# Band masks of a local attention brought to PSUM by 64x64 tiles of the array instead of full 128x128 matmuls

## The reference

```python
def local_attention(q, k, v):
    ...
    sim = jnp.einsum('bhwid,bhwjd->bhwij', bq, bk)
    mask = (i < j) | (i > j + WINDOW) | (j == -1)
    sim = jnp.where(mask, -jnp.finfo(sim.dtype).max, sim)
    attn = jax.nn.softmax(sim, axis=-1)
    out = jnp.einsum('bhwij,bhwjd->bhwid', attn, bv)

def _layer(x, wqkv, qs, ksc, wo, lg, lb, w1, b1, w2, b2):
    q, k, v = jnp.split(shift_token(x) @ wqkv, 3, axis=-1)
    q, k = rotary_xpos(l2norm(q) * qs, l2norm(k) * ksc)
    x = x + local_attention(q, k, v) @ wo
    a, g = jnp.split(layernorm(shift_token(x)) @ w1 + b1, 2, axis=-1)
    return x + (a * gelu(g)) @ w2 + b2

x = x + 0.5 * _L0_ffn_ref(_layernorm(x), ...)
x = x + _L0_attn_ref(_layernorm(x), ...)
x = x + 0.5 * _L0_ffn_ref(_layernorm(x), ...)
```

## Time and profile before

| | |
|---|---|
| median of three runs | 2494.72 us (2492.01 to 2496.49) |
| the profiled execution | 2494.18 us |
| its span in the trace | 2492.4 us |
| mean granted clock of TensorE | 0.952 |
| busy: PE, PE weight loads, DVE, ACT, POOL | 2238.0, 1670.2, 1709.9, 1465.2, 1095.6 us |
| first matmul of q and k in the two calls of the feed-forward stage | 67.63 and 1287.17 us |

### The profile page before, as it was taken

The page is one execution under the profiler, slowest core; times in us unless marked ns, Lnnn a source line. Parts: engine busy times, 40 slices in busy tenths (PEclk is TensorE's granted clock), DMA queues, the critical chain, the costliest instruction groups (busy, mean ns, idle before and its releaser), DMA issues. The chain is left out here.

```text
span 2492.4 us, 52712 instructions
## 1 busy us (share of the span) xinstructions
PE 2238.0 (90%) x21606; PEld 1670.2 (67%) x21606; DVE 1709.9 (69%) x2815; ACT 1465.2 (59%) x2389; POOL 1095.6 (44%) x800
## 2 busy tenths in 40 slices
PE   1799999999999969999969999999999997597968
PEld 1577777777777646666646777777777775495758
DVE  3677777778888636777737777777788784563556
ACT  0476767666676515555546677766676664363635
POOL 4655555656555210000025565656555560550245
PEclk8799999999999969999989999999999998698979
DMA  7000000069999970000000000000000002221022
GB/s 152 1 1 1 2 1 1 1 76 119 131 147 147 147 85 1 2 2 2 2 1 1 2 1 1 1 2 2 1 2 1 1 1 68 55 70 38 33 74 81
DMA packets 211362, 90.88 MB, mean 36 GB/s; under 512 B 79700, under 2 KB 206721, under 8 KB 210996
## 3 DMA queue, kind: packets, MB, share of 16 engines
q1 hardware_dynamic: 202596, 72.27, 21.8%
q0 software_dynamic: 6080, 11.76, 1.5%
q10 hardware_dynamic: 2448, 3.48, 0.7%
HBM read 24.51 MB, written 63.41 MB: 35 GB/s over the span
## 5 line engine op out<-in xcount | busy, mean ns | idle before, releaser
L477 POOL TENSOR_TENSOR work<-work,rot_tables 128x512 f32<-128x512 f32 x256 | 446.5, 1764 | 440.7 <-ACT work L581 440.7
L485 POOL TENSOR_TENSOR work<-work 128x1024 f32<-128x1024 f32 x128 | 305.2, 2384 | 13.0 <-DVE work L911 3.1
L911 DVE TENSOR_TENSOR work<-work,rot_tables 128x1024 f32<-128x1024 f32 x128 | 162.2, 1268 | 112.2 <-ACT work L581 112.2
L1068 DVE TENSOR_REDUCE small<-psum 128x4 f32<-128x1024 f32 x128 | 156.5, 1223 | 95.5 <-PE psum L1584 95.4
L1310 PE MATMUL psum<-qkv_w_hi,h_hi 128*128 128x512 f32 x384 | 182.7, 476 | 18.9 <-POOL h_lo L504 16.4
L1464 PE MATMUL psum<-centered,ffn_w 128*128 128x256 f32 x768 | 190.3, 399 | 6.1 <-DVE centered L972 2.9
L928 DVE TENSOR_TENSOR work<-work,small 128x1024 f32<-128x1024 f32 x128 | 159.5, 1248 | 51.2 <-ACT small L595 47.0
L692 ACT ACTIVATE work<-psum 128x1024 f32<-128x1024 f32 x128 | 131.2, 1025 | 102.2 <-PE psum L1591 102.2
L1402 PE MATMUL psum<-work 64*128 64x128 f32 (+1 forms) x2048 | 180.8, 307 | 0.0
L492 POOL TENSOR_TENSOR y_all<-centered,squared 64x256 f32<-64x256 f32 x64 | 48.7, 761 | 295.0 <-ACT squared L641 292.4
L1464 PEld LDWEIGHTS psum<-centered,ffn_w 128*128 128x128 f32 x768 | 145.8, 196 | 36.2 <-DVE centered L972 17.7
(11 more groups left out here) (285 smaller groups left out, 5718.6 us busy)
## 6 DMA issues: line engine op xcount, KB each, us to landing
h_area<-mean_weights SPq DMA_DIRECT2D x24, 2048.0 KB
tile_x<-h_area SPq DMA_DIRECT2D x39, 128.5 KB, 2.1
stage<-in_consts ACTq DMA_DIRECT2D x1, 3009.0 KB, 12.6
tile_x<-h_area SPq DMA_DIRECT2D x39, 64.5 KB, 1.8
work<-in_x SPq DMA_DIRECT2D x4, 512.0 KB, 27.4
expert_w<-in_ew SPq DMA_DIRECT2D x1, 2048.0 KB, 8.6
expert_w<-in_ew SPq DMA_DIRECT2D x8, 256.0 KB, 6.9
work<-y_tokens SPq DMA_DIRECT2D x4, 512.0 KB, 6.1
```

The costliest lines, as they stand in the source:

```text
L477: last = pool.tensor_tensor(b[:, :, :, o_], a[:, :, :, i_], tab[:, l, 1, t, :, o_].unsqueeze(2).to_broadcast([P, 2, HEADS, 32]), ALU.mult)
L485: pool.tensor_tensor(rC[:, t, :], rC[:, t, :], rB[:, t, :], ALU.add).then_inc(f_sum, 1)
L911: dve.tensor_tensor(g(rC[:, t, :]), g(rA[:, t, :]), tab[:, l, 0, t, :, :].unsqueeze(2).to_broadcast([P, 2, HEADS, DH]), ALU.mult)\
L1068: dve.tensor_reduce(dst, PS[:, 0:2, :].rearrange("p b (t j) -> p b t j", t=TILES), AX, ALU.max, negate=True).then_inc(a_smax, 1)
```

## The change

`masks` gets a second row of halves. `halves_of` puts rows 0 to 63 of the masks in both halves of the partitions, and behind them rows 64 to 127, in both again. So partitions 0 to 63 and 64 to 127 each hold the whole mask, in two pieces side by side. The new `bands` opens each pair of banks by four matmuls of 64x64: row half `r` brings its copy of the mask to bank `bs[r]`, once for output partitions 0 to 63 and once for 64 to 127. Both places call it. To make room in SBUF, the row buffers of the expert stage (`tile_y_sum`, `tile_y`) become parts of `work1`.

```diff
+def halves_of(a):
+
+    return np.concatenate([np.tile(a[0:64], (2, 1)), np.tile(a[64:P], (2, 1))], 1)
...
-    parts = dict(rot=rot, masks=np.concatenate([st0, st1, s0, s1], 1), relu=np.concatenate([relu_pf, relu_fp], 1),
+    parts = dict(rot=rot, masks=halves_of(np.concatenate([st0, st1, s0, s1], 1)), relu=np.concatenate([relu_pf, relu_fp], 1),
...
-        masks = sb("masks_bf", [P, 2 * JW], BF16)
-        mst0, mst1 = masks[:, 0:J0W], masks[:, J0W:JW]
-        ms0, ms1 = masks[:, JW:JW + P], masks[:, JW + P:2 * JW]
+        masks = sb("masks_bf", [P, 2, 2 * JW], BF16)
+        mst0, mst1 = slice(0, J0W), slice(J0W, JW)
+        ms0, ms1 = slice(JW, JW + P), slice(JW + P, 2 * JW)
...
-        ysum = [sb(f"tile_y_sum{n}", [P, D]) for n in range(2)]
-        yrow = [sb(f"tile_y{n}", [P, D]) for n in range(4)]
+        ysum = [work[1][:, 4608 + D * n:4608 + D * (n + 1)] for n in range(2)]
+        yrow = [work[1][:, 4864 + D * n:4864 + D * (n + 1)] for n in range(4)]
...
+            def bands(bs, n, w, m):
+                for half in range(2):
+                    for r, b in enumerate(bs):
+                        k_, o_ = slice(64 * r, 64 * r + 64), slice(64 * half, 64 * half + 64)
+                        pe.matmul(PS[o_, b, 0:n * w], eyeb[k_, k_],
+                                  masks[k_, half, m].unsqueeze(1).to_broadcast([64, n, w]),
+                                  start=True, stop=False, skip_group_check=True)
...
-                        n = len(hs) // 2
-                        for b in bs:
-                            pe.matmul(PS[:, b, 0:n * w], eyeb[:, :], m.unsqueeze(1).to_broadcast([P, n, w]),
-                                      start=True, stop=False, skip_group_check=True)
+                        bands(bs, len(hs) // 2, w, m)
```

More of the change, by code:

```diff
@@ L850, in _ @@
             link(dve.memset(mneg[:, :, :], 0.0))
-            link(dve.tensor_copy(masks[:, :], part("masks")))
+            link(dve.tensor_copy(masks[:, :, :].rearrange("p a n -> p (a n)"), part("masks")))
             link(dve.tensor_copy(relub[:, :, :].rearrange("p a b -> p (a b)"), part("relu")))
@@ L1386, in scores_T, with masked @@
                               ((0, 1), range(4, 8), J0W, 0, 0, mst0))
[L1388 to L1392, removed]
+                    def masked(bs, hs, w, j, i0, m):
+                        bands(bs, len(hs) // 2, w, m)
                     def products(bs, hs, w, j, i0, m):
@@ L1406, in scores_T @@
                     pe.wait_ge(f_cp, min(2 * i + 4, 2 * ITEMS * (f + 1)))
-                    bands(*groups[0])
+                    masked(*groups[0])
                     pe.wait_ge(f_vsb, min(i + 2, ITEMS * (f + 1)))
-                    bands(*groups[1])
+                    masked(*groups[1])
                     pe.wait_ge(f_mTs, i + 1)
@@ L1413, in scores_T @@
                     free(pe, f_u, i)
-                    bands(*groups[2])
+                    masked(*groups[2])
                     products(*groups[2])
```

## The result

| | before | changed |
|---|---|---|
| median of 16 runs, us | 2492.68 | 2480.01 |
| ratio, 95% interval | 1 | 0.9952 (0.9943 to 0.9962) |
| profiled execution, us | 2494.18 | 2480.15 |
| its span, us | 2492.4 | 2478.0 |

The sum came out right. Several of its terms did not, and their errors nearly cancel.

What follows compares the result with a forecast made beforehand. The bound was taken as a circle of waits through DVE, ACT and PE, not PE's busy share. Terms 2.0 + 2.6 + 6.1 + 1.7 - 1.0 gave 11.4 us less than 2494.72, so 2483; range 2474 to 2491.

Steps and rivals of the forecast that it cites:

- The rival by which PE's share decides: Whole item loop: all PE saves counts, 0.68 us an item, 43 us, giving 2451 us; chance 0.03.
- Four tiles at a time: Mask matmuls: four 64x64 tiles stream together, 0.53, 0.37 and 0.16 us for the three places.
- two at a time: Mask matmuls: only two of four tiles overlap, streams as long as before; 14.7 us more, 2509 us; chance 0.07.
- The sign of being wrong that I named, a run over 0.3: Mask run of 384 columns: taking over 0.3 us would show the forecast wrong.
- the two new mode changes: Per item, before the scores' masks and before the transposed masks: 0.10 us each, bounds 0 and 0.20.
- Third group: Third mask group of the transposed scores: 0.095 us saved in all 64 passes, 6.1 us.
- the load and stagger of a run: Start of each mask run: 0.055 us for loading 64 columns and 0.02 for four starts, 0.075 taken.
- First kind: 2.0 + 2.6 us and its part of the 6.1: The 30 passes also normalising the next input: scores 0.07 in 28, first two transposed groups 0.10 in 26, third 0.095.
- The rival that only the third group pays: Item loop: the 2.0 and 2.6 are lost, 6.8 us less, 2487 us; chance 0.13.
- Second kind, scores: The 34 passes where PE waits for the gated product: score masks gain 0, PE idles some 0.4 us longer.
- Ends of the calls: First and last item of each call: 4 x 0.45 + 2 x 0.21 = 2.2 us, 1.7 taken.
- Prologue: Before the item loop: larger constants load 0.5 us and doubled mask cast 0.5, together +1.0 us.

Runs made afterwards that it cites:

- the scores alone: Kernel before with 64x64 tiles only in the masks of the scores, the transposed scores keeping full 128x128 mask matmuls; ratio 0.9992 (0.9977 to 1.0007).
- the repeat: The changed kernel timed once more without edits, beside the one with swapped tile order; ratio 0.9943 (0.9928 to 0.9958) against the kernel before.
- e7: Changed kernel with gelu ahead of the second square, gated product ahead of DVE's last sums, exponentials before reciprocal norms; ratio 0.9994 (0.9981 to 1.0007).

## Why the prediction was right

*The bound.* Right. PE, 98 to 99% busy by the page, was not the bound: it saves 0.41 (scores, 0.507 less a mode change), 0.25 and 0.142, 0.80 us an item, and the passes show 0.14 and 0.18. The rival by which PE's share decides stood at 2451.

*Streaming, loads, modes.* Four tiles at a time was right; 0.67, 0.505 and 0.289 us against 0.53, 0.37 and 0.16 of stream, and the 0.289 is less than the 0.32 that two at a time would stream. The forecast of 0.7 for the scores' run held, the one of 0.33 for the third group's was too long. The sign of being wrong that I named, a run over 0.3, leaves out the mode change behind the run, which the 0.33 contains, so my own forecast would have set it off. Of the two new mode changes the one ahead of the scores is hidden in the second kind: from the start of the last output projection to the first mask PE takes 0.30 before and 0.31 now there, where the first kind has 0.22 and 0.31.

*Third group.* Right in its mechanism, 0.05 short in size: forecast 0.095 x 64 = 6.1 us, measured 0.142 in each pass of the second kind. The step that was off is the load and stagger of a run, 0.075 us from tiles of 128x32. Of the 0.289 us, 0.16 are stream and 0.10 the mode change behind it, so some 0.03 are left for both; 0.668 and 0.505 leave about the same over 0.53 and 0.37. With the 0.02 taken for the starts the load is near the 0.01 of a fast one. The Trainium skill, page "TensorEngine Tiling (Array Packing)", section "Restrictions", has the fast weight load off in column tiles; at 64 bf16 columns no cost of that is seen here. For the 34 passes of the second kind the step gave 3.2 us, the trace 4.8.

*First kind: 2.0 + 2.6 us and its part of the 6.1.* This step failed, though each of its three margins was there. I let the 0.07 of the row maxima, the 0.10 up to the gated product and the third group's 0.095 add up to 0.27, and looked at what binds only as far as the gated product. Beyond it PE meets the second exponential, 0.11 further on. The first two groups and the third share that one margin instead of having one each, so the passes are 0.18 shorter: 4.7 us in the 26 middle passes where 6.9 were forecast. The rival that only the third group pays named such a margin, but laid it to the scores and the first two groups; as it was, the first two groups and the third each give 0.09 alone.

*Second kind, scores.* Right, 0, by the changed kernel and by the scores alone. PE idles 0.50 more before the mean of y; 0.4 was forecast, with a mode change that turned out to be hidden.

*Ends of the calls.* The 60 passes between the first and the last of both calls go from 1461.5 to 1452.4 us, 9.1 less; both calls lose 12.5, so 3.4 belong to the ends, where 1.7 and the third group's 0.4 were forecast. The 0.45 that I gave the scores' masks there is not worked out in the prediction. I halved the first item's part for a delay behind POOL; all of it is lost there. From the first score masks to the end of the subtraction (L951, now L956) the first item of each call takes 7.21 us before and 7.22 now, since the cast ahead of it ends at POOL's end. Up to the attention of the first item the two calls gain 0.3 together, behind that of the last but one 3.1; the repeat has 0.9 and 1.7. So the ends give 2.6 to 3.4 us, most of it at the last items, and why those give more than forecast is open.

*Prologue.* Forecast +1.0, the trace shows +0.14. The profile page's row of the load, and the cast of the masks:

```profile
stage<-in_consts ACTq DMA_DIRECT2D x1, 3329.0 KB, 13.7
```

```profile
34.41 0.23 DVE L854 CAST eye_bf<-eye 128x128 bf16<-128x128 f32 x1 [34.41 <-DMA qk_squares<-in_k_scale]
...
34.92 0.83 DVE L856 CAST masks_bf<-stage 128x1280 bf16<-128x1280 f32 x1
```

The load takes 1.1 us more and hides wholly, as its lower bound had it: DVE is still released by a small load that comes last, here at 34.41 where it was 34.62. The cast takes 0.34 more, not 0.5. 0.34 less 0.21 is 0.13. The first matmul of q and k comes at 67.63 before and 67.77 now, but between 65.7 and 68.7 us in all the traces, so neither the 0.14 nor the forecast of 1.0 can be told from nothing.

Together, against the 11.4: second kind 1.6 more, first kind 2.2 less, ends 1.3 more, prologue 0.9 more, which makes 13.0; the traces of the feed-forward calls with the prologue show 12.4, the medians 12.7. That the sum hit so well is partly luck, since errors of 2 us and more stood on both sides.

## What to carry over

A matmul whose weights are an identity, and which only brings a constant to PSUM, needs no full array: split by rows and columns, two banks at a time, it takes half the stream, at 0.03 us for loads and starts and 0.09 for each new change of mode; splitting by columns alone gives nothing. What a faster engine gains is found by following its starts beyond the next bound to the one after it, here from the gated product to the exponential 0.11 us behind; margins in a row are shared, they don't add. And if only a fifth of the saved engine time shows up, the order of the other engines is the next thing to change: the same edit went from 12.7 to 28.7 us once ACT and DVE did first what PE waited for.

## What the runs showed of the hardware

- A run of four 64x64 tiles is cheap at its start: of its 0.289 us 0.16 are stream and 0.10 the mode change behind it, which leaves 0.03 for everything else, in both loop orders.
- A change of mode costs 0.09 us at the new places, near the 0.10 of the old one: from the start of the last matmul of 128x128 to the first mask it is 0.216 before and 0.309 with quarter or column tiles, ahead of the scores (where PE does not wait) and ahead of the transposed masks. It is a cost even for column tiles that gain nothing, whose scores' and third runs are longer besides (1.205 and 0.448 against 1.175 and 0.431).
- DVE and POOL hold each other up both ways. The cast of 128x32 takes 0.57 beside POOL's L490 and 0.18 in the last item of a call, where POOL has nothing to do. POOL's L482 of 128x512 takes 2.30 when DVE's L916 has started 0.05 before it, and 1.27 beside a reduction, as here in the first order with the gelu ahead (`e7`):

```profile
511.65 1.21 DVE L925 TENSOR_REDUCE small<-qk_squares 128x16 f32<-128x1024 f32 x1
...
511.99 1.27 POOL L482 TENSOR_TENSOR work<-work,rot_tables 128x512 f32<-128x512 f32 x1 [0.86 <-ACT work L586]
```

The Trainium skill, page "SBUF — State Buffer", section "Who interferes with whom", has the shared pair as an exclusive lock, decided by the order of issue, and reductions stay out of it. L916, which reads two tiles of SBUF, still ran 1.18 us when L482 began; 1.18 + 1.27 would be 2.45, so the 2.30 agrees within 0.15.
